# Two attention and feed-forward layers with a router of experts on one core: stack clears placed first or late, the first queries' middle part by a subtraction, fewer ones written, and the engines' orders drawn anew

## What is computed

```python
x = x + L0_xattn(layernorm(x), ctx, ctx, mask, ...)   # 16 heads of 8, relative position bias, mask, softmax
x = x + L0_ffn(layernorm(x), ...)                      # gelu(x U1 V1 + b1) U2 V2 + b2
x = x + L1_xattn(layernorm(x), ctx, ctx, ...)          # 16 heads of 8, softmax, no mask
x = x + L1_ffn(layernorm(x), ...)                      # 16 experts of 64, the best 8 weighted, and one shared
```

## Time and profile before

| | us |
|---|---|
| median of 3 runs (lowest, highest) | 216.0 (214.54, 219.54) |
| the profiled execution's own time | 216.93 |
| its span, first to last instruction | 215.1 |

### The profile page before, as it was taken

One profiled execution on the slowest core, in us unless ns is written; L12 is line 12 of the kernel. 1 busy time (PEld: TensorE's weight loads), 2 busy tenths in 40 slices (PEclk: granted clock), 3 DMA queues, 4 the chain that ended last, 5 costly groups with the idle time before them and its releaser, 6 DMA issues.

```text
span 215.1 us, 4593 instructions
## 1 busy us (share of the span) xinstructions
PE 175.5 (82%) x1609; PEld 121.8 (57%) x1609; DVE 164.6 (76%) x459; ACT 138.5 (64%) x293; POOL 92.2 (43%) x109
## 2 busy tenths in 40 slices
PE   1550626999989789979759696999999999999994
PEld 0320413765556555756624493785676767788883
DVE  4269609969999999798897649599989597878643
ACT  2251404698889989999677948459389888233220
POOL 8186698699579969767123115110200011011000
PEclk9999955699999999999996978599999999999999
DMA  5352388214113650031200231200000100000000
GB/s 139 83 110 72 85 225 178 58 42 109 42 49 78 207 189 3 16 74 26 54 2 12 68 77 37 71 23 23 2 3 2 30 3 0 3 24 0 25 4 24
DMA packets 21879, 12.21 MB, mean 57 GB/s; under 512 B 3120, under 2 KB 21232, under 8 KB 21856
## 3 DMA queue, kind: packets, MB, share of 16 engines
q1 hardware_dynamic: 19776, 10.68, 19.6%
q10 hardware_dynamic: 2080, 1.24, 2.3%
HBM read 4.98 MB, written 0.54 MB: 26 GB/s over the span
## 4 chain that ended last, share of the span: by engine, by line
PE 55%; DVE 23%; ACT 5%; POOL 5%; issue 5%; SPq 2%; DMA 2%; ACTq 1%; DVEq 0%
PE bank L460 15%; PE bank L489 9%; PE bank L403 6%; PE bank L359 4%; PE bank L343 4%; DVE es L884 4%; PE bank L374 3%; DVE mx L893 3%; PE bank L439 2%; DVE q0p L1030 2%; SPq L211 2%; PE bank L476 2%; DVE x L934 2%; PE bank L429 2%; DVE ct L923 2%
## 5 line engine op out<-in xcount | busy, mean ns | idle before, releaser
L1766 POOL TENSOR_TENSOR es<-es,mx 128x512 f32<-128x512 f32 x32 | 33.6, 1065 | 8.0 <-DVE mx L889 7.8
L1744 POOL TENSOR_TENSOR rstd<-ve,half 128x2 f32<-128x2 f32 x16 | 11.1, 694 | 57.0 <-DVE ve L872 56.8
L1486 ACT ACTIVATE gth<-bank 128x256 f32<-128x256 f32 (+1 forms) x36 | 13.4, 382 | 24.6 <-PE bank L460 23.9
L403 PE MATMUL bank<-pt,va 128*32 128x128 f32 x512 | 27.3, 297 | 1.7 <-DVE es L884 0.6
L374 PE MATMUL bank<-ident,es 128*128 128x128 f32 x128 | 20.4, 291 | 4.6 <-ACT es L1426 2.9
L460 PE MATMUL bank<-xT,wg 128*128 128x256 f32 (+1 forms) x72 | 23.8, 414 | 0.0
L893 DVE TENSOR_REDUCE mx<-bank 128x4 f32<-128x512 f32 x32 | 20.5, 677 | 3.1 <-PE bank L359 3.1
L884 DVE TENSOR_TENSOR es<-bank,biasq 128x512 f32<-128x512 f32 x32 | 20.7, 679 | 2.1 <-PE bank L359 2.1
L460 PE MATMUL bank<-xT,wu 128*128 128x256 f32 (+1 forms) x72 | 21.9, 386 | 0.0
L489 PE MATMUL bank<-wd,hT 128*128 128x128 f32 x128 | 21.2, 289 | 0.0
L1426 ACT ACTIVATE es<-es 128x512 f32<-128x512 f32 x32 | 19.2, 624 | 2.8 <-POOL es L1766 2.8
(11 more groups left out here) (140 smaller groups left out, 359.4 us busy)
## 6 DMA issues: line engine op xcount, KB each, us to landing
k0st<-k0p SPq DMA_DIRECT2D x24, 64.0 KB, 2.0
k1st<-k1p SPq DMA_DIRECT2D x24, 64.0 KB, 2.0
q1st<-q1p SPq DMA_DIRECT2D x24, 64.0 KB, 2.0
q0st<-q0p SPq DMA_DIRECT2D x21, 64.0 KB, 2.0
biasq<-rel_bias_scratch SPq DMA_DIRECT2D x4, 256.0 KB, 5.2
wu<-in_wu SPq DMA_DIRECT2D x1, 544.0 KB, 3.9
wg<-in_wg SPq DMA_DIRECT2D x1, 544.0 KB, 4.9
x<-in_x SPq DMA_DIRECT2D x4, 128.0 KB, 3.7
```

The costliest lines, as they stand in the source:

```text
L403: ins = pe.matmul(dst[32 * s:32 * s + VW, h // 4 * SEQ:(h // 4 + 1) * SEQ], va[:, p, b, l, VCOLS * h:VCOLS * h + VW], pt[:, l, b, h], star ...
L1766: pool.tensor_tensor(es[:, b, h], es[:, b, h], mx[:, 0, p, b, h].unsqueeze(2).broadcast_to([128, 4, SEQ]), ALU.subtract).then_inc(nth(f"le ...
```

## The change

- Clears. GpSimd clears both k0st buffers at the very start (before: the second after the first keys' parts), q1st0 after the first parts, q1st1 to q1st3 behind the second pair's queries, and the two k1st buffers between the first pair's `less_least`. VectorE clears both q0st buffers at the very start.
- The first pair's middle query part is `whole - first` written in bfloat16 by a TENSOR_TENSOR, instead of a cast of the rest; the rest is computed after it.
- `value_ones` writes only the columns of va that no value is copied into: the 24 columns at each row's end, and one column of each head's nine.
- TensorE projects queries first (q0, k0, k1 instead of k0, k1, q0), and nearly all of the five lists are in another order.

```diff
             def values(l, p, b, c, k=None):
-                new(pe, "va_ones", 1) and pe.wait_ge(sem("va_ones"), 1)
+                new(pe, "va_ones", 2) and pe.wait_ge(sem("va_ones"), 2)
...
-            project("k0", 0, 2)
-            project("k1", 0, 3)
-            project("q0", 0, 4)
+            project("q0", 0, 2)
+            project("k0", 0, 3)
+            project("k1", 0, 4)
...
+            def first_queries_middle():
+
+                freed(dve, "q0.0")
+                dve.tensor_tensor(parts["q0"][0][:, 1], whole["q0"][0][:], parts["q0"][0][:, 0], ALU.subtract).then_inc(nth("q0_first", 0), 1)
+
             def first_queries_rest():
-                freed(dve, "q0.0")
+                new(dve, "q0_first", 1) and dve.wait_ge(sem("q0_first"), 1)
                 dve.tensor_tensor(whole["q0"][0][:], whole["q0"][0][:], parts["q0"][0][:, 0], ALU.subtract).then_inc(nth("q0_first_rest", 0), 1)
 
-            def first_queries_middle():
+            def first_queries_last():
                 new(dve, "q0_first_rest", 1) and dve.wait_ge(sem("q0_first_rest"), 1)
-                dve.tensor_copy(parts["q0"][0][:, 1], whole["q0"][0][:]).then_inc(nth("q0_first", 0), 1)
-
-            def first_queries_last():
-                new(dve, "q0_first", 1) and dve.wait_ge(sem("q0_first"), 1)
                 dve.tensor_tensor(parts["q0"][0][:, 2], whole["q0"][0][:], parts["q0"][0][:, 1], ALU.subtract).then_inc(nth("q0_first", 1), 1)
...
             def value_ones():
-                pool.memset(va[:], 1.0).then_inc(nth("va_ones", 0), 1)
+
+                sums = va[:, :, :, :, 0:HEADS * VCOLS].rearrange("p i b l (h v) -> p (i b l) h v", v=VCOLS)
+                pool.memset(va[:, :, :, :, HEADS * VCOLS:].rearrange("p i b l e -> p (i b l) e"), 1.0).then_inc(nth("va_ones", 0), 1)
+                pool.memset(sums[:, :, :, DK], 1.0).then_inc(nth("va_ones", 1), 1)
```

More of the change, by code:

```diff
@@ new lines, in _ @@
+            values(0, 0, 1, 1)
+            scores0(1, 0, 0, 5, 0)
+            scores0(1, 0, 2, 2, 1)
+            front_turned(2, 7)
+            values(0, 0, 1, 2)
+            weights_turned(0, 1, 3, 5)
+            scores0(1, 1, 0, 0, 2)
+            value_rows(2, 0, 7)
+            value_rows(2, 1, 5)
+            values(0, 0, 1, 3)
+            front_turned(3, 7)
+            project("q0", 2, 1)
+            scores0(1, 1, 2, 5, 0)
+            project("q0", 3, 7)
+            project("k0", 2, 6)
@@ new lines, in _ @@
+            weights_turned(3, 0, 1, 6)
+            weights_turned(3, 0, 2, 1)
+            scores1(0, 0, 0, 7, 2)
+            attention_out(0, 2, 3)
+            weights_turned(3, 0, 3, 6)
+            values(0, 3, 0, 1)
+            scores1(0, 0, 2, 1, 0)
+            weights_turned(3, 1, 0, 3)
+            values(0, 3, 0, 2)
+            weights_turned(3, 1, 1, 6)
+            values(0, 3, 0, 3)
+            values(0, 3, 1, 0, 3)
+            tokens_turned(2, 1, 6)
+            values(0, 3, 1, 1)
@@ L663, in _ @@
+            weights_turned(3, 1, 2, 7)
+            scores1(0, 1, 0, 5, 6)
+            project("q1", 1, 2)
+            tokens_turned(1, 2, 1)
+            values(0, 3, 1, 2)
+            scores1(0, 1, 2, 7, 0)
+            weights_turned(3, 1, 3, 5)
+            ffn_up(2, 0, 2)
+            max_turned(0, 0, 1)
+            ffn_up(2, 1, 6)
+            values(0, 3, 1, 3)
+            gate_turned(5)
+            ffn_down(2, 0, 7)
+            max_turned(0, 1, 0)
             ffn_down(2, 1)
+            attention_out(0, 3, 2)
@@ new lines, in _ @@
+            gate_up(0, 4, 5)
+            scores1_turned(2, 0, 0, 6, 7)
+            scores1_turned(2, 0, 2, 2, 4)
+            attention_out(1, 1, 0)
+            gate_up(0, 5, 1)
+            gate_up(0, 6, 3)
+            max_turned(2, 1, 5)
+            gate_up(0, 7, 6)
+            gate_up(0, 8, 0)
+            scores1(3, 0, 0, 7, 2)
+            combine_turned(0, 5)
+            values(1, 2, 0, 0, 4)
+            values(1, 2, 0, 1)
+            values(1, 2, 0, 2)
+            spread(0, 0, 7)
@@ new lines, in _ @@
+            spread(1, 2, 1)
+            values(1, 3, 0, 1)
+            attention_out(1, 2, 0)
+            values(1, 3, 0, 2)
+            max_turned(3, 1, 2)
+            down(1, 0, 6)
+            values(1, 3, 0, 3)
+            spread(1, 3, 7)
+            down(1, 1)
+            spread(1, 4, 0)
+            spread(1, 5, 1)
+            spread(1, 6, 2)
+            down(1, 2)
+            gate_up(1, 6, 7)
+            down(1, 3)
+            tokens_turned(3, 2, 4)
+            scores1_turned(3, 1, 0, 5, 3)
@@ L1088, in _ @@
             clear("q0", 0)
+            clear("q0", 1)
             variance(0, 0)
             mask_values()
+            shift(0, 0)
             rel_rows()
-            shift(0, 0)
             cast_ident()
@@ L1416, in copy_values @@
             def copy_values(p, b):
-                new(act, "va_ones", 1) and act.wait_ge(sem("va_ones"), 1)
+                new(act, "va_ones", 2) and act.wait_ge(sem("va_ones"), 2)
                 src = read(act, f"v.{p}{b}")
@@ L1807, in _ @@
             less_least(0, 0, 1)
-            power(0, 2)
+            last_part("k0", 1)
+            clear("k1", 0)
             less_least(0, 0, 2)
+            clear("k1", 1)
             less_least(0, 0, 3)
@@ L1813, in _ @@
             less_least(0, 1, 2)
+            power(0, 2)
             less_least(0, 1, 3)
-            first_rest("q0", 2)
+            power(0, 3)
+            first_rest("k1", 1)
             residual(0, 0)
@@ L1949, in _ @@
             stack(sp, "k1", 1, 2)
+            stack(sp, "k1", 2, 2)
             max_rows(sp, 1, 0)
-            stack(sp, "k1", 2, 2)
             stack(sp, "q1", 0, 2)
```

928 lines of the change are left out of this document (425 added, 503 removed).

## The result

The changed kernel took 203.0 us (median of four runs, 201.4 to 204.6) against 216.2 us for the kernel before on the same chip (214.5 to 219.5): a ratio of 0.939, 95% interval 0.929 to 0.949. Run again beside another batch it took 202.4 us (201.0 to 203.5, six runs) against 215.5.

A forecast was written before the change was run, and what follows sets the result against it. The start, up to about 37 us, was taken as bound by a chain through VectorE's stalled cast and GpSimd's clears. 5.9 us carried plus 0.5 for the order, 6.4 off 216.0, gave 209.6 us; range 204.4 to 215.5.

The forecast's parts named there:

- The cast and the second front: Start: queries first and the subtraction free the second pair's turned front, xcT at 16.0 instead of 20.48; gain 4.5 us.
- The next step: GpSimd from xcT to the first `less_least`: query and key parts end at about 20.95 instead of 26.09; gain 6.7 us.
- Clears, ones, the first pair: GpSimd's start: ones 0.6 us, first `less_least` at 26.3, fourth at 33.6, first pair ended at 39.4.
- The second pair's first `less_least` at 43.5: GpSimd behind the first pair: this mark comes at 43.5 instead of 49.43, gain 5.9 us.
- the rival that has TensorE take GpSimd's place: TensorE, full ahead of the second pair's first transpose, leaves 0 to 4 us of the 6.4: 212 to 216; chance 0.18.
- I carry the 5.9 us through unchanged: Rest of the program: same instructions in another order, same TensorE work, so the early 5.9 us reach the end.
- 0.5 us for the order: Rest of the program: 0.5 us added for the order's care for VectorE's waits.
- upper bound of 2.3 us: Most the order term could give, if it also closed a third of TensorE's 5.4 us of holes from 110 to 140 us.
- a rival in which they cost time at 1.2 GHz: Early stretch and passage between layers: 16 us more at low clock would cost 6.8 us, outweighing the gain; chance 0.08.
- the same rows priced it at 5.7 us: TensorE between 110 and 140 us: 13.4 us at 1.2 GHz, busy for 0.85 of it, lost some 5.7 us.
- it lasts as long: Experts' part: starts some 6 us earlier and takes the same time as before.
- better luck with the clock: Whole program: some 2.6 us allowed at the range's fast end, beside 6.7 and 2.3, giving 204.4.

The follow-up runs named there:

- a_order: The changed kernel with its three local edits undone (cast, ones over all of va, clears in their old places), its orders kept: 209.0 us, ratio 0.965.
- a_cast: The changed kernel with the cast of before in place of the subtraction (rest, cast, last): 204.0 us median.
- a_clears: The changed kernel with every clear back in its old place, subtraction and short ones kept: 207.6 us (207.3 to 210.5).
- cut by cut: The changed kernel's lists up to some 97, 110, 118 or 127 us, the order of before behind: 214.4, 210.4, 207.1 and 208.1 us.

## Why the prediction was wrong in size

*The cast and the second front: right.* The cast waited for the clears and the subtraction didn't; xcT came at 15.4 for 16.0. (The next step's terms, from 17.9 us on, add up to 20.75 and not 20.95; nothing hangs on it.) But the step counted the subtraction as what removes the stall. Queries first does it as well (0.29 us for the cast in a_order and in a_cast), so the edits overlap. The Trainium skill ("SBUF — State Buffer", "Who interferes with whom") was borne out in both halves: the cast was blocked beside clears and free beside an idle GpSimd. And two-input instructions of VectorE beside GpSimd's subtractions took 1.19 and 1.16 us for a mask addition of 0.69, GpSimd's own 0.85 to 1.11 for 0.67. These half microseconds lay in the slack that the step had given them.

*Clears, ones, the first pair: right*, each mark within 0.8 us. By a_clears the clears' places are worth 4.6 to 5.2 us at the end.

*The second pair's first `less_least` at 43.5: missed in this profile* (46.7), hit within 1 us in others (42.8, 44.4). I gave no price to TensorE at 1.2 GHz between 22 and 42 us, though the rival that has TensorE take GpSimd's place described the spot. It took 3 us of the lead at that mark. After 637 matmuls the changed kernel was 5.3 us ahead all the same, so the lead was not lost, and the carried 5.9 us were near the truth.

*"I carry the 5.9 us through unchanged", and 0.5 us for the order: the step that failed.* The term of 0.5 us was mis-sized: instead of it the rest of the program gave 7.0 in the profiles, 3.2 in the 340 matmuls of the passage and 3.8 in the last 632. From 98 us on the argument looked at nothing but the earlier trace rows. Of its upper bound of 2.3 us, 1.8 were a third of the 5.4 us of holes between 110 and 140 us; of those, 2.8 closed. Two things are missing beside that. The clock: I gave the lists behind 98 us a rival in which they cost time at 1.2 GHz, and none in which they take away what before has, though the same rows priced it at 5.7 us. How much of it was won stays open. And the experts' part, for which the prediction said that it lasts as long: at equal work its order is worth 1.5 to 2.5 us.

*The range* was built from one-sided bounds: up to the rivals, down by 2.6 us of "better luck with the clock". With the 5.7 us itself in place of the 2.6 it would have reached 201.3 and held the result. That would have been luck in part, since no run shows that the clock alone gives 5.7 us. By the fastest runs alone, 8.9 us apart, the forecast of 6.4 was off by less than by the medians.

What stays open: which of the moves behind 98 us does what. No single one that was tried (maximum rows, turned scores) gave anything, and cut by cut the medians move by 3 to 5 us (once by 1 the wrong way), where the runs of one cut kernel differ by 3 to 9 among themselves. Nor is it known how much of the 7.0 us goes by the clock.

## What to carry to other kernels

When whole lists are drawn anew, don't carry a gain through as a constant. Price every later stretch by the idle time and the low clock that it has now, in both directions, and let the range reach to what they hold. Compare traces at equal work (matmuls done), not at the start of a phase, which a new order moves. A cast that stalls beside GpSimd's clears can be cured by an order that gives it an idle GpSimd, and then an edit to the cast itself was worth nothing that could be told.

## What the runs showed of the hardware

- A profile's clock record can be incomplete. That of the changed kernel shows 1.00 throughout, while pairs of matmuls take 1.22 us at 29 us and 0.56 at 46.
- The kernel before spreads over 9.6 us between runs of the same program, and the granted clock orders most of them; the changed kernel, with 28.8 us of holes instead of 39.6, spreads over 3.6.
- A 128x256 cast on VectorE took 4.99 us beside three clears of GpSimd and 0.29 us beside an idle GpSimd. As a subtraction it took 0.42 us in the changed kernel and 0.65 in the kernel before with that one edit.
- Strided writes of GpSimd cost little here: 256 single columns of ones took 0.55 us and 384 in runs of 24 took 0.41 us, where all 2,688 had taken 2.34.
